# First stage with softplus spread between maxima, rows placed one batch back and TensorE's loop turned; experts on 28 pairs of tiles, then 15 single tiles

## The chip, the core and the metric

One core of a Trainium2 chip runs the whole program in one launch. The metric is the device time of that execution in microseconds. The kernel before was timed at 1516.23 us (median of three runs).

## What is computed

A block of three residual layers over 128 sequences of 32 rows of 256 numbers (4096 rows in all), in float32.

```python
x = x + cross_attention(layernorm(x), ctx)     # ctx: 128 x 257 x 256, 16 heads of 16
x = x + ssd_layer(layernorm(x))                # dt = softplus(...); cumulative sums; conv; W_out
# mixture of experts, z = layernorm(x), 8 experts, 256 -> 704 -> 256, the best 2 for each row
logits = z @ w_router.T
top_w, sel = jax.lax.top_k(logits, 2)
gates[row, sel] = softmax(top_w)
for e in range(8):
    h = silu(z @ w_gate[e]) * (z @ w_up[e])
    out = out + gates[:, e:e+1] * (h @ w_down[e])
x = x + out
```

## The kernel before

The program has two blocks, and all engines run each from lists written out by hand. Everything is ordered by semaphores: an instruction waits until a counter has reached a value. In loops the value depends on the loop's register, so a wait can cost the engine's sequencer an instruction of its own.

**First stage** (`attend`). The rows are worked in 32 tiles of 128 rows; a tile holds 4 sequences, called batches b = 0 to 3 (n = 4i + b). `steps` writes tiles 0 to 3 out, runs tiles 4 to 28 as a hardware loop of 25 turns, and writes the rest out. Several batches are in flight at once. While batch n has its values weighed (`weigh_values`, L412 with output `k`), the probabilities of n + 1 are turned (`transpose_probs`, outputs `pt` and `v_p` at L476), and keys and values of n + 2 are projected (`project_k`, `project_v`, outputs `k` and `v_p`). The scores (output `sc`) of n + 1 stand at the head of batch n's piece of the list. Between these stand small steps of the layers behind (`turn_a`, `turn_b`, `turn_c`: outputs `m`), one per gap. Each matmul of a context or expert product is done three times, high by high, high by low and low by high part (fp32r operands), so that the result is nearly float32.

VectorE takes the maximum of each group of scores (`maxima`, L884), copies the keys out of PSUM (`take_keys`, L873), takes reciprocals (L891), and does the small vector work of the other layers: softplus by a series in L977 to L1003 (its last product, L1003, gives `a_done`, which TensorE's scores of batch 1 wait for, since the series has its scratch in the second bank of scores), the placement of routed rows in L1080 to L1102 (`place`), queries in L923 and the layer norms. ScalarE does the exponentials and PSUM copies, GpSimd the low parts of the context (`ctx_lo`), the powers and the indirect DMAs; SyncE issues plain DMAs.

At the end `plan_tiles` works out on VectorE which expert each tile of 128 table rows belongs to, in a chain of 10 small operations, and writes it to `info`.

**Second stage** (`experts`). 71 tiles of up to 128 routed rows, each of one expert, run two per loop turn (`tiles`, `body`). For each tile GpSimd copies the tile's column of the table (`gi`, `oi` at L1664), gathers the rows by an indirect DMA (L1670) and later adds the result to the output by another (L1676, `scatter`, which waits until the one before has landed); TensorE turns the rows (`z_p`, L1480, 2 transposes), multiplies them by the gate and up weights (`gate_p`, `up_p`: rows stationary, weights moving, 24 matmuls of 352 columns), turns the product `h` (`ht_p`, L1513, 6 transposes), and multiplies by the down weights (`y_p`, 18 matmuls of 256 columns). ScalarE and VectorE split the weights of the tile's expert into high and low parts anew for every tile (`gw`, `uw`: L1553 on ScalarE, L1611 on VectorE, 1408 numbers a partition each). The low part of the down weights comes by DMA (768 KB a tile).

Of the kernel before, what the change touches and what calls it, by code (L numbers as in the profile page):

```python
# [4 lines left out]
F32 = mybir.dt.float32  # L5
# [7 lines left out]
P = 128  # L13
# [20 lines left out]
NSLOT = (TOK * TOPK + E * (P - 1)) // P  # L34
assert NSLOT % 2 == 1
# [42 lines left out]
def perceiver(nc, xd, ctxd, ctxl, maskd, pard, wxbcd, cond, padd, wgd, wud, wdd, outd):  # L78
# [5 lines left out]
    with keep:  # L84
# [8 lines left out]
        info = keep.enter_context(nc.sbuf_tensor("info", [P, 2, NSLOT + 1], I32))  # L93
# [21 lines left out]
def attend(nc, xd, ctxd, ctxl, maskd, pard, wxbcd, cond, padd, wgd, wud, wdd, d_high, d_low, zbuf, table, outd, con, cst, wg, wu, wd,  # L115
# [7 lines left out]
    with own:  # L123
# [11 lines left out]
        cnti = sb("cnti", [P, E], I32)  # L135
        past = sb("past", [P, 2, E])
        tl = sb("tl", [P, 5])
# [134 lines left out]
        PLAN = 10  # L272
# [137 lines left out]
        def _(pe):  # L410
# [15 lines left out]
            def project_k(i, b):  # L426
# [4 lines left out]
                at_least(pe, k_done, 2 * n)  # L431
                at_least(pe, ou_done, n - 2)
                at_least(pe, rp_done, n - 2)
# [7 lines left out]
            def project_v(i, b):  # L441
                n = 4 * i + b
                hi, lo = ctx_hi[:, b % 2], ctx_lo[:, b % 2]
                at_least(pe, v_done, n)
                at_least(pe, pt_done, 2 * n - 2)
# [7 lines left out]
            def scores(i, b):  # L453
                n = 4 * i + b
                pe.wait_ge(qbd_done, n + 1)
                pe.wait_ge(k_done, 2 * n + 2)
                pe.wait_ge(last_done, n + 1)
                at_least(pe, max_done, 4 * n)
# [8 lines left out]
            def transpose_probs(i, b, d):  # L467
                n = 4 * i + b
                pe.wait_ge(exp_done, 4 * n + 2 * d + 2)
                at_least(pe, pt_done, 2 * n)  # L470
# [8 lines left out]
            def weigh_values(i, b):  # L479
                n = 4 * i + b  # L480
                pe.wait_ge(pt_done, 2 * n + 2)
                pe.wait_ge(v_done, n + 1)
                if runs(following(i, b, 2)[0]):
                    pe.wait_ge(k_done, 2 * n + 6)
                at_least(pe, ou_done, n)
                at_least(pe, rp_done, n)
# [181 lines left out]
            def tile(i):  # L668
                for b in range(TB):
                    nxt, two = following(i, b), following(i, b, 2)  # L670
                    if runs(nxt[0]):
                        scores(*nxt)
# [10 lines left out]
                    if runs(nxt[0]):  # L683
                        transpose_probs(*nxt, 1)

# [14 lines left out]
            turn_z1(1)  # L700
            steps(pe, tile)
# [4 lines left out]
            for k in range(2):  # L706
                last = mm(M[0:1, (k + 1) * P:(k + 2) * P], tl[:, 3 + k:4 + k], ident)
# [156 lines left out]
        def _(dve):  # L864
# [104 lines left out]
            def link(ins, j, k):  # L969

                ins.then_inc(soft, 1)
                dve.wait_ge(soft, NSOFT * j + k)

            def softplus_ratio(j):
                dve.wait_ge(u_done, j + 1)
                dve.wait_ge(soft_max, j + 1)
                link(V.tensor_scalar(sr, su, 2.0, None, ALU.add), j, 1)  # L977
                link(V.reciprocal(ss, sr), j, 2)
                V.tensor_tensor(sy, su, ss, ALU.mult).then_inc(soft, 1)
                V.tensor_tensor(sp_y, su, ss, ALU.mult).then_inc(soft, 1)  # L980

            def softplus_series(j, first, last):

                if first == 0:
                    dve.wait_ge(soft, NSOFT * j + 4)
                    link(V.tensor_tensor(sw, sp_y, sy, ALU.mult), j, 5)
                    V.tensor_scalar(ss, sw, 1.0 / ATANH[0], None, ALU.mult).then_inc(soft, 1)
# [117 lines left out]
            def plan_tiles():  # L1105
# [3 lines left out]
                def link(ins):  # L1109
                    k[0] += 1  # L1110
                    ins.then_inc(plan, 1)
                    if k[0] < PLAN:
                        dve.wait_ge(plan, k[0])

                number = cst("tok")[:, 0:1]
                dve.wait_ge(cnt_ready, 1)
                link(V.tensor_scalar(cnti[:, :], M[:, 0:E], float(P - 1), None, ALU.add))
                link(V.tensor_scalar(cnti[:, :], cnti[:, :], P.bit_length() - 1, None, ALU.logical_shift_right))
                link(V.tensor_copy(cnt[:, 0, :], cnti[:, :]))
                link(V.tensor_tensor_scan(cnt[:, 1, :], ones[:, 0:E], cnt[:, 0, :], 0.0, ALU.mult, ALU.add))  # L1120

                link(V.tensor_scalar(past[:, 0, :], cnt[:, 1, :], number, None, ALU.is_le))
                link(V.tensor_tensor(past[:, 1, :], past[:, 0, :], cnt[:, 0, :], ALU.mult))
                link(V.tensor_reduce(tl[:, 0:2], past[:, :, :], AX.X, ALU.add))
                link(V.tensor_tensor(tl[:, 2:3], number, tl[:, 1:2], ALU.subtract))
# [637 lines left out]
```

## Time and profile before

| | us |
|---|---|
| median of 3 runs | 1516.23 |
| lowest, highest | 1511.95, 1516.65 |
| the profiled execution, its own time | 1514.07 |
| its span, first to last instruction | 1512.0 |
| TensorE busy | 1418.8 (94%) |
| VectorE, ScalarE, GpSimd busy | 1119.2, 1002.8, 833.8 |

The page cuts the span into 40 equal slices; the first stage reaches to about 1000 us, the experts follow. TensorE's matmuls are pipelined, so a matmul's duration is longer than its turn: starts of successive matmuls give the pace. Durations are of one execution, on one core.

### The profile page before, as it was taken

What the parts mean: (1) busy time and instruction counts of PE and PEld (TensorE: products, weight loads), DVE (VectorE), ACT (ScalarE), POOL (GpSimd) and SP (SyncE); (2) the same over time, 40 slices, a digit from 0 to 9 for tenths busy, and PEclk for the clock granted to TensorE, in tenths of its full rate; (3) what the DMA queues carried; (4) which work ended last, traced back from release to release, by engine and by line L of the source; (5) the groups of instructions that cost most, each with busy time, mean ns of one, the idle gap of its engine ahead of it and who ended that gap; (6) DMA issues with size and microseconds to landing.
All of it is one profiled execution on the core that took longest, in us unless ns stands there. A gap on an engine that the chain in (4) does not pass through costs nothing.

```text
span 1512.0 us, 54304 instructions
## 1 busy us (share of the span) xinstructions
PE 1418.8 (94%) x15668; PEld 1285.3 (85%) x15669; DVE 1119.2 (74%) x3999; ACT 1002.8 (66%) x2482; POOL 833.8 (55%) x1401
## 2 busy tenths in 40 slices
PE   6969999999999999999999999559999999999997
PEld 5858888888888888888888888459999999999997
DVE  3647877877877877877877877558777777787775
ACT  4626777677777767767767766147767677677674
POOL 3514655655655665665665654236666656566554
PEclk9969999999999999999999999569999999999999
DMA  6202454454343343343343231425555555555554
GB/s 189 71 21 72 139 180 129 145 186 129 104 112 91 100 116 91 97 119 91 92 120 95 83 83 31 183 97 145 160 145 151 155 143 159 136 144 162 143 143 111
DMA packets 102009, 183.81 MB, mean 122 GB/s; under 512 B 19392, under 2 KB 61376, under 8 KB 101792
## 3 DMA queue, kind: packets, MB, share of 16 engines
q1 hardware_dynamic: 86272, 164.35, 35.8%
q0 software_dynamic: 15680, 18.76, 7.0%
q8 instruction: 29, 0.48, 0.1%
q14 instruction: 28, 0.23, 0.0%
HBM read 152.63 MB, written 31.13 MB: 122 GB/s over the span
## 4 chain that ended last, share of the span: by engine, by line
PE 70%; DVE 10%; issue 7%; DMA 2%; POOL 2%; ACT 1%; DVEq 1%; POOLq 0%; ACTq 0%; SPq 0%
PE k L412 12%; PE m L412 10%; PE y_p L1474 9%; PE up_p L1474 9%; PE gate_p L1474 8%; PE v_p L412 6%; PE sc L412 5%; PE v_p L476 4%; PE pt L476 3%; PE ht_p L1513 3%; DVE kT L873 2%; DMA par<-zbuf,gi 2%; PE m L497 2%; DVE z L1031 1%; PE z_p L1480 1%
## 5 line engine op out<-in xcount | busy, mean ns | idle before, releaser
L738 ACT ACTIVATE wd<-wd,nmx 128x257 f32<-128x257 f32 x512 | 256.3, 504 | 35.3 <-DVE nmx L884 30.6
L714 ACT ACTIVATE wd<-v_p 128x512 f32<-128x512 f32 x256 | 152.6, 596 | 180.8 <-PE k L412 146.3
L884 DVE CUSTOM_DVE_ANT_0 wd<-sc,wd 128x257 f32<-128x257 f32 x512 | 192.2, 423 | 74.2 <-PE sc L412 69.5
L1301 POOL TENSOR_TENSOR ctx_lo<-wd,ctx_hi 128x516 fp32r<-128x516 f32 x128 | 166.9, 1304 | 138.3 <-ACT ctx_hi L714 138.3
L1676 POOL DMA_INDIRECT out<-par,oi x71 | 113.6, 1599 | 144.8 <-ACT par L1582 140.0
L412 PE MATMUL k<-ctx_hi,wkh 128*128 128x256 f32 x512 | 159.0, 311 | 1.7 <-POOL ctx_lo L1301 1.4
L1553 ACT ACTIVATE uw_hi<-wu 128x1408 fp32r x71 | 98.4, 1385 | 83.7 <-PE up_p L1474 83.4
L1664 POOL COPY oi<-par 128x4 int32 x71 | 148.1, 2086 | 0.0
L1611 DVE TENSOR_TENSOR uw_lo<-wu,uw_hi 128x1408 fp32r<-128x1408 f32 x71 | 115.5, 1626 | 41.2 <-ACT uw_hi L1553 41.2
L412 PE MATMUL k<-ctx_lo,wkh 128*128 128x256 f32 x512 | 145.4, 284 | 0.0
L412 PE MATMUL k<-ctx_hi,wkl 128*128 128x256 f32 x512 | 144.7, 283 | 0.0
L1611 DVE TENSOR_TENSOR gw_lo<-wg,gw_hi 128x1408 fp32r<-128x1408 f32 x71 | 115.4, 1625 | 39.2 <-ACT gw_hi L1553 39.2
L412 PE MATMUL v_p<-wvh,ctx_lo 128*128 128x256 f32 x512 | 143.8, 281 | 0.0
L412 PE MATMUL v_p<-wvh,ctx_hi 128*128 128x256 f32 x512 | 143.4, 280 | 0.0
L412 PE MATMUL v_p<-wvl,ctx_hi 128*128 128x256 f32 x512 | 142.8, 279 | 0.0
L873 DVE TENSOR_SCALAR kT<-k,par 128x256 f32<-128x256 f32 x256 | 114.0, 477 | 31.1 <-PE k L412 30.4
L1664 POOL COPY gi<-par 128x4 int32 x71 | 122.4, 1723 | 9.2 <-issue 5.6
L1474 PE MATMUL y_p<-wd,hT_hi 128*128 x426 | 120.8, 284 | 1.9 <-DVE hT_lo L1611 1.9
L1474 PE MATMUL y_p<-wd,hT_lo 128*128 x426 | 120.1, 282 | 0.0
L1474 PE MATMUL y_p<-dl,hT_hi 128*128 128x256 f32 x426 | 119.8, 281 | 0.0
L1319 POOL TENSOR_TENSOR rr<-wd,rr 128x4 f32<-128x4 f32 x128 | 25.7, 201 | 165.4 <-DVE rr L891 165.1
L1553 ACT ACTIVATE gw_hi<-wg 128x1408 fp32r x71 | 98.1, 1382 | 13.9 <-PEq L123 8.8
(200 smaller groups left out, 4719.2 us busy)
## 6 DMA issues: line engine op xcount, KB each, us to landing
dl<-d_low SPq DMA_DIRECT2D x71, 768.0 KB, 4.4
wd<-in_ctx SPq DMA_DIRECT2D x128, 258.0 KB, 2.8
wd<-in_mask SPq DMA_DIRECT2D x512, 32.1 KB, 1.8
wd<-in_wd SPq DMA_DIRECT2D x24, 256.0 KB, 3.0
d_high<-wd SPq DMA_DIRECT2D x24, 256.0 KB
d_low<-wd SPq DMA_DIRECT2D x24, 256.0 KB
wd<-d_high SPq DMA_DIRECT2D x8, 768.0 KB, 9.2
wg<-in_wg SPq DMA_DIRECT2D x8, 704.0 KB
```

The costliest lines, as they stand in the source:

```text
L412: return nc.tensor.matmul(out, lhsT, rhs, start=start, stop=stop)
L476: last = nc.tensor.transpose((PT, V_)[d][:, o:o + P], pr[:, g, t * P:(t + 1) * P], ident)
L714: return nc.scalar.activation(out, in_, ACT.Copy, **kw)
L738: nc.scalar.activation(pr[:, g, :], sm[:, g, :], ACT.Exp, bias=nmx[:, g:g + 1], scale=-1.0, accum_out=rsum[:, g:g + 1]).then_inc(exp_done, 1)
L873: V.tensor_scalar(kT[:, b % 2, a, 0:LAST], K2[:, a, :], prm("bk")[:, a:a + 1], None, ALU.add).then_inc(k_done, 1)
L884: V.tensor_tensor_reduce(sm[:, g, :], SC[g][:, 0:S], msk[:, b, :], -1.0, 3.0e38, ALU.add, ALU.min, nmx[:, g:g + 1]).then_inc(max_done, 1)
L1301: G.tensor_tensor(ctx_lo[:, b % 2], ctx[:, b], ctx_hi[:, b % 2].bitcast(F32), ALU.subtract).then_inc(lo_done, 1)
L1474: return nc.tensor.matmul(out, lhsT, rhs, start=start, stop=stop)
L1553: nc.scalar.activation(dst, src, ACT.Copy).then_inc(done, 1)
L1611: V.tensor_tensor(dst, src, hi.bitcast(F32), ALU.subtract).then_inc(done, 1)
L1664: G.tensor_copy(dst.unsqueeze(1), tab[:, bass.ds(col, 1), :]).then_inc(done, 1)
L1676: G.indirect_dma_start(outd[:, :], bass.IndirectOffsetOnAxis(oi[:, s, 1:2].bitcast(U32), 0), yb[:, s, :], None, compute_op=ALU.add).then_i ...
```

## The change

The change has four parts.

1. **TensorE's loop is turned.** In the first stage's list the scores of batch n + 2 now stand at the end of batch n's piece, and the scores of (0, 1) are written ahead of the tiles. The order of matmuls stays as it was; only the place in it where the loop branches back moves, from ahead of the scores to behind them. Waits that other waits imply are left out.
2. **Softplus is spread.** In batch 3 VectorE's softplus chain (`softplus_ratio`, `softplus_series`) is cut so that each of its first steps stands between two maxima or key copies, and the rest of the series stands behind the key copies.
3. **`place` goes from batch 2 to batch 1**, ahead of `normalise2`.
4. **Experts in pairs.** The first 28 steps of the second stage take two tiles of one expert (256 rows); 15 single tiles follow, by the code of before with other buffers. `plan_tiles` gives both lists in 25 operations. In a pair the weights are stationary and the 256 rows move: 5 full chunks of 128 hidden units (12 matmuls of 256 columns each) and a short one, gate and up side by side (6 matmuls). The product comes out with hidden units on partitions, so `h` is not turned. The weights are split once for a pair. The down product has 36 matmuls of 256 columns.

```diff
             def tile(i):                     # TensorE, first stage
                 for b in range(TB):
                     nxt, two = following(i, b), following(i, b, 2)
-                    if runs(nxt[0]):
-                        scores(*nxt)
                     turn_c(*((i, b - 1) if b else (i - 1, TB - 1)))
...
                     if runs(nxt[0]):
                         transpose_probs(*nxt, 1)
+                    if runs(two[0]):
+                        scores(*two)
...
                     if runs(nxt[0]):          # VectorE, first stage
                         maxima(*nxt, 0, 1)
                     if soft_now:
-                        softplus_ratio(i - 1)
+                        softplus_add(i - 1)
                     if runs(nxt[0]):
                         maxima(*nxt, 2)
                     if soft_now:
-                        softplus_series(i - 1, 0, 1)
+                        softplus_inverse(i - 1)
                     if runs(nxt[0]):
                         maxima(*nxt, 3)
+                    if soft_now:
+                        softplus_ratio(i - 1)
...
-                    if b == 2 and runs(i - 3):
-                        place(i - 3)
...
+                    if b == 1 and runs(i - 3):
+                        place(i - 3)
...
+            def chunk(p, s, k):               # TensorE, experts
+                at_least(pe, hf_done, FC * p + k - 2)
+                (zh, zl), (wh, wl) = zT2[s], w2
+                for side in range(1 if k == FULL else 2):
+                    o = 2 * k * P + side * P
+                    for c in range(NH):
+                        for j, (w, z) in enumerate(((wh, zh), (wh, zl), (wl, zh))):
+                            last = mm(G2[k % 3][:, side * F2:(side + 1) * F2], w[:, c, o:o + P], z[:, c, :],
+                                      c == 0 and j == 0, c == NH - 1 and j == 2)
+                last.then_inc(gu_ready, 1)
...
+            def body2(p, s):
+                chunk(p, s, 0)
+                chunk(p, s, 1)
+                if not (isinstance(p, int) and p == 0):
+                    down_pair(p - 1, 1 - s)
+                if final(p):
+                    turn_z(0, 0)
+                else:
+                    turn_pair(p + 1, 1 - s)
+                for k in range(2, FC):
+                    chunk(p, s, k)
...
+            def take_y2(p, s, h):             # ScalarE
+                act.wait_ge(yp_ready, 2 * p + h + 1)
+                act.wait_ge(oi_done, p + 1)
...
+            def scatter_pair(p, s):           # GpSimd
+                for h in range(2):
+                    held(pool, (tab_in, 16), (oi_done, p + 1), (yp_done, 2 * p + h + 1), (y_out, 16 * (2 * p + h)))
+                    G.indirect_dma_start(outd[:, :], bass.IndirectOffsetOnAxis(oi[:, s, h, 1:2].bitcast(U32), 0),
+                                         yb2[:, h, :], None, compute_op=ALU.add).then_inc(y_out, 16)
```

For each chunk of a pair ScalarE takes silu of the gate half from PSUM (`silu2`), VectorE multiplies by the up half (`gate_up2`), ScalarE rounds the product to its high part (`high_h`) and VectorE takes the low part (`low_h`); each step waits for the one before.

TensorE's list at the head of the loop of the first stage, before the change (`v_p` at L476 is the last transpose of batch 3, the branch is L282, `sc` the scores of the next tile's batch 1):

```order
L476 MATMUL v_p<-con,wd 128x128 [waits v_done,pt_done,exp_done]
L476 MATMUL v_p<-con,wd 128x128 x3
L282 REGISTER_ALU
L282 COMPARE_AND_BRANCH
L412 MATMUL sc<-kT,qbd 64x257 [waits max_done,last_done,a_done,k_done,qbd_done]
L412 MATMUL sc<-kT,qbd 64x257 x7
L412 MATMUL m<-dtv,con 128x16 [waits a_done,z1T_done]
```

The same place in the changed kernel, whose lines are numbered anew:

```order
L484 MATMUL v_p<-con,wd 128x128 [waits v_done,exp_done]
L484 MATMUL v_p<-con,wd 128x128 x3
L466 REGISTER_ALU
L420 MATMUL sc<-kT,qbd 64x257 [waits a_done,last_done,k_done]
L420 MATMUL sc<-kT,qbd 64x257 x7
L290 REGISTER_ALU
L290 COMPARE_AND_BRANCH
L420 MATMUL m<-dtv,con 128x16 [waits a_done,z1T_done]
```

The branch has moved behind the scores, and the scores have two waits fewer.

VectorE's list in batch 3, around the key copies, before (L884 maxima, L979 to L990 softplus, L873 the two key copies):

```order
L979 TENSOR_TENSOR dtv<-dtv,sc 128x16 [waits soft]
L980 TENSOR_TENSOR sc<-dtv,sc 128x16
L884 ISA wd,nmx<-sc,wd 128x257 [waits s_ready,init]
L884 ISA nmx 128x1
L986 TENSOR_TENSOR dtv<-sc,dtv 128x16 [waits soft]
L987 TENSOR_SCALAR sc<-dtv 128x16 [waits soft]
L884 ISA wd,nmx<-sc,wd 128x257 [waits s_ready,init]
L884 ISA nmx 128x1
L990 SCALAR_TENSOR_TENSOR sc<-sc,dtv 128x16 [waits soft]
L873 TENSOR_SCALAR kT<-k,par 128x256 [waits k_ready,s_ready]
L990 SCALAR_TENSOR_TENSOR sc<-sc,dtv 128x16 [waits soft]
L873 TENSOR_SCALAR kT<-k,par 128x256 [waits k_ready,s_ready]
```

And after (L892 maxima, L988 to L1002 softplus, L881 key copies, L899 the reciprocals):

```order
L892 ISA wd,nmx<-sc,wd 128x257 [waits s_ready,init]
L892 ISA nmx 128x1
L988 TENSOR_TENSOR dtv<-dtv,sc 128x16 [waits soft]
L989 TENSOR_TENSOR sc<-dtv,sc 128x16
L881 TENSOR_SCALAR kT<-k,par 128x256 [waits k_ready,s_ready]
L993 TENSOR_TENSOR dtv<-sc,dtv 128x16 [waits soft]
L881 TENSOR_SCALAR kT<-k,par 128x256 [waits k_ready,s_ready]
L999 TENSOR_SCALAR sc<-dtv 128x16 [waits soft]
L1002 SCALAR_TENSOR_TENSOR sc<-sc,dtv 128x16 [waits soft] x2
L899 RECIPROCAL rr<-rsum 128x4 [waits px_done,exp_done]
L1002 SCALAR_TENSOR_TENSOR sc<-sc,dtv 128x16 [waits soft] x4
```

Of the chain from the ratio (L979, now L988) on, six operations stood ahead of the second key copy; now three do, and seven follow it.

GpSimd's list of one single-tile step in the loop of the experts, before (L1664 the copies of the table's columns into `gi` and `oi`, L1670 the gather, L1676 the scatter):

```order
L1664 COPY oi<-par 128x4
L75 REGISTER_ALU
L1663 ISA [waits zT_ready]
L1663 TENSOR_LOAD info
L1663 ISA x2
L1664 ISA
L1664 COPY gi<-par 128x4
L66 REGISTER_ALU
L1670 DMA par<-zbuf,gi 128x256 [waits gi_done,tab_in]
L66 REGISTER_ALU
L1676 DMA out<-par,oi 4224x256 [waits y_done,y_out,oi_done,tab_in]
```

And of one pair step, after (L2007 the gathers, L1999 the copy into `oi`, L2014 the scatters):

```order
L68 REGISTER_ALU
L2007 DMA par<-zbuf,gi 128x256 [waits gi_done,tab_in]
L2007 DMA par<-zbuf,gi 128x256
L1998 ISA
L1998 TENSOR_LOAD info
L1998 ISA x2
L1999 ISA
L1999 COPY oi<-par 128x8
L68 ISA
L2014 DMA out<-par,oi 4224x256 [waits yp_done,y_out,oi_done,tab_in]
L68 ISA
L2014 DMA out<-par,oi 4224x256 [waits yp_done,y_out,oi_done,tab_in]
```

Before, a step had a copy of each kind, one gather and one scatter; now it has the same two copies, twice as wide, two gathers and two scatters, and the second scatter waits until the first has landed (`y_out`).

## Rows read from the trace of the kernel before

**Rows 1.** Two windows, one in each stage: span, then busy us per engine, clock, DMA.

```profile
500.00:900.00 400.00, 390.52 (x5308) 339.12 (x5307) 314.42 (x1554) 282.04 (x869) 233.93 (x492) 1.00 0.35 99
...
1000.00:1500.00 500.00, 489.92 (x3524) 485.94 (x3525) 387.75 (x423) 353.49 (x493) 299.02 (x278) 0.99 0.55 145
```

**Rows 2.** Timeline of TensorE in a looped tile: start, us, instructions, idle before.

```profile
608.13 0.66 PE L476 MATMUL pt<-con,wd 128*128 128x128 f32 x4
...
608.98 0.62 PE L412 MATMUL m<-par,z2T 128*128 128x16 f32 x4 [0.19 <-DVE wd L923]
...
614.46 0.65 PE L412 MATMUL k<-wd 128*32 128x64 f32 x32 [0.20 <-DVE kT L873]
...
616.00 0.63 PE L476 MATMUL v_p<-con,wd 128*128 128x128 f32 x4
...
616.88 0.69 PE L412 MATMUL sc<-kT,qbd 32*64 32x257 f32 x16 [0.26 <-issue]
...
622.29 0.66 PE L476 MATMUL pt<-con,wd 128*128 128x128 f32 x4
...
622.78 0.29 PE L412 MATMUL m<-dtv,con 128*128 128x16 f32 x2
```

**Rows 3.** The same view in a tile written out after the loop.

```profile
872.12 0.63 PE L476 MATMUL v_p<-con,wd 128*128 128x128 f32 x4
...
872.68 0.69 PE L412 MATMUL sc<-kT,qbd 32*64 32x257 f32 x16
```

**Rows 4.** Timeline of VectorE over the tile of rows 3.

```profile
858.09 0.41 DVE L1037 TENSOR_SCALAR z<-x,mv,rs 128x256 f32<-128x256 f32 x1 [1.58 <-POOL rs L1285]
...
863.19 0.16 DVE L1080 TENSOR_REDUCE sv<-ohr 128x2 f32<-128x16 f32 x1
...
864.26 0.15 DVE L1102 SCALAR_TENSOR_TENSOR ri<-ri,sv 128x2 int32<-128x2 int32 x1
...
870.05 0.48 DVE L873 TENSOR_SCALAR kT<-k,par 128x256 f32<-128x256 f32 x1
...
872.25 0.16 DVE L1003 TENSOR_TENSOR dtv<-sc,par 128x16 f32<-128x16 f32 x1
```

**Rows 5.** Timeline of TensorE over one expert tile.

```profile
1202.22 0.28 PE L1474 MATMUL y_p<-wd,hT_hi 128*128 x1
...
1204.36 0.82 PE L1513 MATMUL ht_p<-con 128*128 128x128 f32 x6
...
1205.18 0.32 PE L1474 MATMUL gate_p<-gw_lo,zT_hi 128*128 128x352 f32 x1
...
1206.79 0.32 PE L1474 MATMUL gate_p<-gw_hi,zT_lo 128*128 128x352 f32 x1
...
1207.33 0.32 PE L1474 MATMUL up_p<-uw_lo,zT_hi 128*128 128x352 f32 x1
...
1211.24 0.82 PE L1513 MATMUL ht_p<-con 128*128 128x128 f32 x6
```

**Rows 6.** Waits of TensorE in the expert stage: us in total, times, longest.

```profile
PE z_p L1480 <- DMA par<-zbuf,gi: 6.6, 4, 2.9
```

**Rows 7.** Groups of the expert stage: busy us, mean ns, idle before.

```profile
L1611 DVE TENSOR_TENSOR hT_lo<-ht_p,hT_hi 128x256 fp32r<-128x256 f32 x71 | 29.4, 415 | 0.0
...
L1553 ACT ACTIVATE hT_hi<-ht_p 128x256 fp32r<-128x256 f32 x71 | 26.9, 379 | 0.0
```

**Rows 8.** Timeline of GpSimd over the tile of rows 5.

```profile
1203.18 1.00 POOL L1670 DMA_INDIRECT par<-zbuf,gi  x1 [0.80 <-POOL gi L1664]
...
1205.94 1.60 POOL L1676 DMA_INDIRECT out<-par,oi  x1 [1.76 <-ACT par L1582]
...
1207.57 1.67 POOL L1664 COPY gi<-par 128x4 int32 x1
```

**Rows 9.** DMA issues by line: KB each where known, median us to landing.

```profile
out<-par,oi POOLq DMA_INDIRECT x71, 3.9
```

More of the change, by code:

```diff
@@ L1405, in experts @@
[L1405 to L1411 removed]
+        F2 = 2 * P
@@ new lines, in experts, with part, cut @@
+        FULL = FC - 1
+        GU = 2 * FULL * P + 2 * FL
+        SPLIT_A, SPLIT_B = 2, 4
+        ZW, HK, WW = 2 * NH * F2, 2 * (FC + 2) * F2, 2 * NH * GU
+        places = dict(w=WW, z0=ZW, z1=ZW, x=768, ht=HK, dl=FC * D)
+        begin, at = {}, 0
+        for name, n in places.items():
+            begin[name] = at
+            at += n
+        room = sb("room", [P, at], F32R)
+        def part(name, skip, n):
+            return room[:, begin[name] + skip:begin[name] + skip + n]
+        def cut(name, skip, *shapes):
+            out = []
+            for shape in shapes:
+                n = 1
+                for k in shape:
+                    n *= k
+                names = " ".join("abcd"[:len(shape)])
+                sizes = {"abcd"[k]: shape[k] for k in range(len(shape))}
+                out.append(part(name, skip, n).rearrange(f"p ({names}) -> p {names}", **sizes))
+                skip += n
+            return out
@@ L1437, in flat, with pairs @@
             return part.rearrange("p c n -> p (c n)")
+        def pairs(eng, body):
+            body(0, 0)
+            body(1, 1)
+            with eng.Fori(2, NPAIR - 2, 2) as p:
+                body(p, 0)
+                body(p + 1, 1)
+            body(NPAIR - 2, 0)
+            body(NPAIR - 1, 1)
         def tiles(eng, body):
@@ L1659, in _, with pair_owners, gather_pair @@
             G = nc.gpsimd
+            def pair_owners(dst, p, done):
+                col = G.value_load(info[0:1, 0, bass.ds(p, 1)], min_val=0, max_val=TCOL - 2)
+                G.tensor_copy(dst, tab[:, bass.ds(col, 2), :]).then_inc(done, 1)
+            def gather_pair(p, s):
+                if not (isinstance(p, int) and p < 2):
+                    pool.wait_ge(z_ready, p - 1)
+                pair_owners(gi[:, s], p, gi_done)
+                held(pool, (tab_in, 16), (gi_done, p + 1))
+                for h in range(2):
+                    G.indirect_dma_start(zg2[:, s, h, :], None, zbuf[:, :],
+                                         bass.IndirectOffsetOnAxis(gi[:, s, h, 0:1].bitcast(U32), 0)).then_inc(zg_in[s], 16)
```

518 lines of the change are left out of this document (382 added, 136 removed).

## The prediction

> **What bounds the kernel now.** I read the table of windows first, to see whether each stage has one limit. It has: TensorE is busy 390.5 of 400 us in a stretch of the first stage and 489.9 of 500 in one of the experts, at full clock, while VectorE has 314 and 388, ScalarE 282 and 353, GpSimd 234 and 299 [rows 1]. So an edit pays by matmul time that it takes out, or by the small holes between matmuls. I looked for those in TensorE's timeline, taking starts of successive groups, because matmuls overlap. Then VectorE's timeline, for what is late ahead of each hole; then the experts' timeline of TensorE and of GpSimd, whose serial loop is the nearest other limit of a pair.
>
> **Turned loop.** Where the loop branches, the scores start 0.88 us after the last value transposes (616.00 to 616.88) [rows 2]; in a tile written out, with the same matmuls and no branch, 0.56 [rows 3]. The branch costs 0.32. Behind the scores it has their 0.69 us of matmuls to hide under; I leave 0.1 exposed, since it still has to be fetched and the next instruction waits on counters. The Trainium skill ("Advanced Engine Details and Errata", "Control Flow Timing") puts a compare-and-branch at about 108 ns; by that the part would give some 3 us over 25 turns, not 8. The rows show three times that, and they decide, since the branch brings register work with it. The dropped waits I cost at nothing: with or without a branch, the 0.56 holds them.
>
> **Softplus spread.** TensorE waits 0.20 for the keys at 614.46 [rows 2], because six softplus operations stand ahead of VectorE's second key copy. With three there, that is gone. What is late next is the end of the series: the product at L1003 ended at 872.41, and the scores of batch 1 wait for it, which started 872.68 (872.25 + 0.16) [rows 3, 4]. The slack is 0.27 there, and about 0.59 in the loop, where the branch held the scores back. VectorE's work ahead of that product is the same, so it ends when it did, and with 0.32 and 0.20 taken from TensorE's way only 0.07 of slack is left. I give 0.05 back for it. Boundary: 0.32 + 0.20 - 0.1 - 0.05 = 0.37; 25 turns make 9.3 us. In the written-out tiles only the key wait goes, some 0.1 each, 0.7 in all.
>
> **Place moved.** In batch 2 the queries of L923 are late, because `place` (863.19 to 864.41, 1.2 us [rows 4]) stands ahead: from `pt` to the next group 0.85 us instead of the usual 0.49 (608.13 to 608.98, against 622.29 to 622.78) [rows 2], so 0.36 are lost a tile. In batch 1 it goes ahead of the normalise, before which VectorE stands idle for 1.58 us waiting for GpSimd's powers [rows 4]: 1.2 fits, if its own inputs are there. That idle is the cover; without it the 1.2 would delay L1037 and, two groups on, TensorE. Of the 0.36 I take 0.24, since the value transposes wait for ScalarE's copy anyway: 28 tiles, 6.7 us. In the last tiles, where the pipeline is thin, `place` also leaves the chain: 1 to 2 us. **First stage: 9.3 + 0.7 + 6.7 + 1.3 = 18.** Bounds: 5 (only half of each hole comes free) and 25 (all of 0.52 and 0.36, 13 + 10, and the tail).
>
> **Pairs.** One tile takes 6.88 us of TensorE (`ht_p` to `ht_p`, 1204.36 to 1211.24), two 13.76. From the rows: 18 down matmuls of 256 columns start over 2.14 us (1202.22 to 1204.36), 0.119 each. Gate matmuls of 352 columns take 0.161 (ten from 1205.18 to 1206.79). The 0.54 to the first up matmul hold two of these and two transposes: 0.22 for the transposes. The six transposes of `h` take 0.82 - 0.16 = 0.66 [rows 5].
> A pair has 5 x 12 + 6 = 66 matmuls of 256 columns for gate and up, and 36 for down: 102 x 0.119 = 12.14. Four transposes of rows: 0.44. Sum 12.6; the saving is 1.16 a pair, of which 2 x 0.66 is turned `h` that no longer exists; the columns that stream are as many as before (102 x 256 = 26,112 = 2 x (24 x 352 + 18 x 256)). Times 28: -32.5 us. That is the ceiling.
> What eats of it: each chunk of 1.43 us (12 x 0.119) has a chain behind it of silu, product, high part, low part, four steps that I price by the 256-wide 379 ns of ScalarE and 415 ns of VectorE [rows 7]: about 1.6 us plus hand-offs. Three buffers of PSUM let it lag two chunks, 2.86 us, and the last chunk's chain must be over within chunks 0 and 1 of the next pair. It fits, by about a microsecond at each chunk and by some 0.3 at the end if VectorE and ScalarE have weight splits queued. Neither engine gets fuller: VectorE was busy 78% of the stretch, 10.7 us for two tiles, ScalarE 71%, 9.7 [rows 1], and the split of the weights is now done once instead of twice.
> GpSimd is closer. Its cycle for a pair is serial: first scatter issued, landed, second scatter issued, then a copy of `gi`, two gathers, a copy of `oi`. With 1.6 a scatter, 1.0 a gather [rows 8], 3.9 from issue to landing [rows 9], 0.8 idle ahead of a gather [rows 8], about 0.5 for ScalarE's last evacuation and 0.9 of waiting and issue at each scatter (half of the 1.76 there [rows 8], the rest being ScalarE's lateness), and 2.35 for the two gathers: 0.5 + 0.9 + 3.9 + 0.9 + 1.6 + 0.8 + 2.35 = 10.95, and two copies. A copy can last 0.2 or 1.67 [rows 8]: 11.3 to 14.4. TensorE gives it 12.6. I take a pace of 12.8: (13.76 - 12.8) x 28 = **-27**.
> Why a copy of 4 numbers takes 1.67 us only sometimes, the profile doesn't say. The Trainium skill ("SBUF — State Buffer", "SBUF: two separate sides") has the port that VectorE and GpSimd share as an exclusive lock, held for the whole of a VectorE operation with two SBUF inputs while GpSimd reads SBUF. By that rule more of them in a pair speak against this change. The long copy fits it, the trace doesn't prove it; with both copies long the cycle is 14.4 and the pairs lose half a microsecond each.
>
> **Gathers, start, transition.** TensorE waited 6.6 us for gathers in four places [rows 6]; 43 steps with the gather a longer step ahead keep perhaps 1.5: -5. Against that the start of the experts is later by about 2 (a second gather of 1.0 ahead of the first matmul, wider splits of weights, four transposes for two). From the last pair to the first single tile its last chain (about 1.6 plus hand-offs) has no chunks to hide under, then the single tile starts cold: +3.5. Fifteen single tiles run as before. `plan_tiles` has 15 operations more of about 0.15 us (the small ones of [rows 4]), covered by the table's way to memory and back; uncovered they are +2.
>
> **Sum.** -18 - 27 - 5 + 2 + 3.5 = -44.5. The profiled execution took 1514.07 us: 1469.6. The median lies 2.2 above it, so I say 1472.
>
> **Rivals.**
> A, the forecast: TensorE sets the pace of pairs at 12.6 to 12.9, first stage -10 to -25: 1460 to 1480 (at best, all bounds together and start and transition at 3: 1516 - 25 - 32.5 - 6.6 + 3 = 1455). Chance 0.55.
> B, pairs paced by GpSimd's serial cycle at 13.0 to 13.7. For: two scatters that wait for one another, one of two copies long. Against: TensorE's 12.6 lies above the low half of the cycle's range, and an expert's gather runs a pair ahead. 28 x 0.5 = 14 less saved: 1475 to 1495. 0.25.
> C, the first stage gives nothing: the end of softplus (L1003) takes the place of the branch and the keys. For: it ended 0.27 ahead of the scores [rows 3, 4], and nothing moves it forward. Against: the 0.36 of `place` is another batch. With pairs dense: 1516.2 - 27 - 5 + 5.5 = 1490. 0.10.
> D, slower: the cycle of B passes 13.76, the time of two single tiles. It needs both copies long and the scatter's landing above 3.9 on wide pairs. The first stage and the gathers bring 23, less 2 + 3.5 is 17.5, so the sign turns at a cycle of 13.76 + 17.5 / 28 = 14.4; at 15.5 the pairs lose 28 x 1.74 = 49, less 17.5: about 1547. 0.06. Between 14.2 and 14.55 it is no change that can be told: 0.04.
>
> **Numbers.** Likeliest: 1472. A measurement of this kernel tells about 0.3% from no change, 4.5 us. Faster 0.90 (A, B, C), same 0.04, slower 0.06. For 8 in 10 the range takes A, most of B and C: 1453 to 1500.
>
> **What would show it.** After: `sc` at the head of batch 1 about 0.56 behind the last `v_p` and the branch's hole under 0.15 behind it; `k<-wd` without a wait for `kT`; L923's wait gone, and L1037 no later than before. In the experts 28 pairs 12.6 to 12.9 apart with TensorE's waits on silu and low parts under 0.2 each; if they are further apart, the chain of waits goes through `yb2`, the scatters and the `oi` copy (B, D), or through `hf_done` (the chunks' chain). Wrong would be: 12.6 missed with GpSimd idle, which would mean that the hand-offs of chunks are dearer than 0.3; or a first stage that didn't move.

## The result: 1.3% faster, less than half of what was forecast

The changed kernel took 1496.84 us (median of 4), the kernel before 1516.44: a ratio of 0.9873 with a 95% interval of 0.9855 to 0.9891, 19.6 us less. The forecast was 1472, 44 us less. The profiled execution has a span of 1494.8 us.

The windows of the changed kernel, in the columns of [rows 1]: one in the first stage, one in the pairs.

```profile
500.00:900.00 400.00, 399.44 (x5480) 351.91 (x5478) 328.01 (x1604) 290.32 (x906) 240.62 (x505) 1.00 0.36 99
1000.00:1340.00 340.00, 329.17 (x2571) 311.56 (x2570) 220.46 (x460) 215.19 (x509) 142.65 (x145) 1.00 0.40 94
```

The first stage is denser than before (399.4 of 400 us against 390.5), the pairs are not (329.2 of 340 is 96.8%, against 98.0% of before). So the change gained in one stage and lost in the other. Laid on a clock (the profiled execution of each kernel): TensorE's first gate matmul of the experts came at 1003.0 us before and at 976.6 now, 26.4 earlier. The experts then took, from there to the start of the last matmul, 502.2 us before and 512.5 now, 10.3 more. That makes 16.1; the end behind the last matmul is 1.1 shorter, which gives the 17.2 between the two spans, and the rest to 19.6 is the difference between single executions and medians.

**First stage.** TensorE's timeline in a looped tile, the places of [rows 2]:

```profile
593.47 0.66 PE L484 MATMUL pt<-con,wd 128*128 128x128 f32 x4
593.96 0.52 PE L420 MATMUL m<-par,z2T 128*128 128x16 f32 x4
594.33 0.64 PE L484 MATMUL v_p<-con,wd 128*128 128x128 f32 x4
...
599.07 0.65 PE L420 MATMUL k<-wd 128*32 128x64 f32 x32
...
599.70 0.65 PE L484 MATMUL pt<-con,wd 128*128 128x128 f32 x4
...
600.61 0.63 PE L484 MATMUL v_p<-con,wd 128*128 128x128 f32 x4
601.17 0.69 PE L420 MATMUL sc<-kT,qbd 32*64 32x257 f32 x16
601.79 0.40 PE L420 MATMUL m<-dtv,con 128*128 128x16 f32 x2
```

No wait is left in it. The queries' group follows `pt` after 0.49 us (0.85 before), the keys' group has no wait for `kT`, and the scores follow the value transposes after 0.56 (0.88 before). The first matmul behind the branch follows the scores after 0.62, which is the scores' own length: the branch has gone out of sight wholly. Matmul by matmul, a turn is shorter by 0.33 us at the branch, 0.27 at the keys and 0.46 at the queries, and lasts 27.37 instead of 28.47.

VectorE's timeline around the moved `place` (L1092 to L1114) and the normalise behind it:

```profile
612.96 0.14 DVE L1092 TENSOR_REDUCE sv<-ohr 128x2 f32<-128x16 f32 x1
...
614.16 0.15 DVE L1114 SCALAR_TENSOR_TENSOR ri<-ri,sv 128x2 int32<-128x2 int32 x1
614.64 0.41 DVE L1049 TENSOR_SCALAR z<-x,mv,rs 128x256 f32<-128x256 f32 x1 [0.33 <-POOL rs L1314]
```

Its 1.35 us fill the idle time that stood ahead of the normalise: 1.58 in [rows 4], 0.33 here.

**Pairs.** TensorE's timeline over one pair, from the transposes of the next pair's rows to those of the one after:

```profile
1109.08 0.66 PE L1605 MATMUL all_p<-con,par 128*128 128x128 f32 x4
1109.49 8.15 PE L1596 MATMUL all_p<-room 128*128 128x256 f32 x66
1118.38 0.38 PE L1596 MATMUL all_p<-wd,room 128*128 x1 [0.74 <-DVE room L1884]
...
1120.12 0.59 PE L1596 MATMUL all_p<-wd,room 128*128 x2
1120.55 0.28 PE L1596 MATMUL all_p<-room 64*128 64x256 f32 x1
1120.67 0.59 PE L1596 MATMUL all_p<-wd,room 64*128 x2
1121.10 0.28 PE L1596 MATMUL all_p<-room 128*128 128x256 f32 x1
...
1122.63 0.59 PE L1596 MATMUL all_p<-wd,room 128*128 x2
...
1123.39 0.66 PE L1605 MATMUL all_p<-con,par 128*128 128x128 f32 x4
```

A pair lasts 14.31 us here and 13.8 in the next one; the two lengths alternate, with a mean of 14.05 over twenty pairs. Before, two single tiles took 13.76 [rows 5]. Two things were not in the forecast's sum. First, ahead of the down product TensorE waits 0.74 us for VectorE's low part of `h` (L1884). Second, matmuls of 64 rows stand in the down product. Where the count of active rows changes, the start lies 0.21 us behind the one before, and the one after that again 0.22, instead of 0.12 (1120.12, a group of two of which the second is the first of 64 rows, then 1120.55, in the rows "64*128"). Added up from start to start over 17 pairs, a pair has 12.6 us of matmuls and transposes as forecast, 0.74 for four changes of rows, 0.58 of waits, and 0.1 of rest.

**Ends of the pairs.** TensorE's timeline from the last pair to the single tiles:

```profile
1369.10 0.38 PE L1596 MATMUL all_p<-wd,room 128*128 x1 [2.57 <-DVE room L1884]
...
1379.58 0.85 PE L1694 MATMUL all_p<-con 128*128 128x128 f32 x6 [1.10 <-issue]
...
1388.00 0.69 PE L1612 MATMUL all_p<-con,par 128*128 128x128 f32 x2 [5.66 <-DMA par<-zbuf,gi]
```

There are three waits of 2.57, 1.10 and 5.66 us, 9.3 together, where 3.5 were allowed for. The chain of work that ended last names the third:

```profile
1373.07 6.47 DMA out<-par,oi
...
1382.62 1.70 POOL gi L2032
...
1385.14 2.81 DMA par<-zbuf,gi
...
1388.00 0.69 PE all_p L1612 x2
```

In GpSimd's list the gather for single tile 2 stands behind the last pair's two scatters, and the second of these waits for the first to land (6.47 us, where [rows 9] have a median of 3.9).

**GpSimd in the pairs**, its timeline over the same pair:

```profile
1110.31 1.63 POOL L2014 DMA_INDIRECT out<-par,oi  x1 [2.80 <-ACT par L1781]
1114.96 1.58 POOL L2014 DMA_INDIRECT out<-par,oi  x1 [3.02 <-DMA out<-par,oi]
1115.98 0.77 POOL L1999 COPY gi<-par 128x8 int32 x1
1117.58 1.02 POOL L2007 DMA_INDIRECT par<-zbuf,gi  x1 [0.83 <-POOL gi L1999]
1118.90 1.36 POOL L2007 DMA_INDIRECT par<-zbuf,gi  x1 [0.30 <-issue]
1120.27 0.51 POOL L1999 COPY oi<-par 128x8 int32 x1
1124.66 1.63 POOL L2014 DMA_INDIRECT out<-par,oi  x1 [3.88 <-ACT par L1781]
```

From the first scatter to the end of the `oi` copy are 10.5 us, and then it is idle for 3.88, waiting for ScalarE's scaled rows. Its serial cycle does not set the pace, and the copies are short (0.77 and 0.51; 1.67 in [rows 8]).

### The profile page after: what moved, and what is told of

It reads as the page before. It is cut to its first block, busy times and chain, and to the rows that moved or that the text cites. A ratio compares the mean times of both kernels' runs of the same rounds, so it can differ in the third digit from the quotient of the medians.

```text
span 1494.8 us, 53378 instructions
## 1 busy us (share of the span) xinstructions
PE 1404.7 (94%) x15840; PEld 1263.0 (84%) x15841; DVE 1071.7 (72%) x4211; ACT 964.0 (64%) x2678; POOL 756.3 (51%) x1345
## 4 chain that ended last, share of the span: by engine, by line
PE 81%; issue 3%; DVE 3%; ACT 2%; DMA 2%; POOL 1%; DVEq 1%; POOLq 0%; ACTq 0%; SPq 0%
PE all_p L1596 26%; PE k L420 16%; PE m L420 12%; PE v_p L420 11%; PE sc L420 5%; PE pt L484 4%; PE v_p L484 4%; PE m L504 2%; PE all_p L1605 1%; DMA par<-zbuf,gi 1%; ACT room L1731 1%; DVE con L1913 1%; DVE room L1884 1%; DMA out<-par,oi 0%; DVEq L1922 0%
## 5 line engine op out<-in xcount | busy, mean ns | idle before, releaser
L1596 PE MATMUL all_p<-room 128*128 128x256 f32 (+1 forms) x2634 | 415.8, 292 | 1.8 <-issue 1.5
L1596 PEld LDWEIGHTS all_p<-room 128*128 128x128 f32 x2634 | 364.2, 193 | 2.6 <-issue 2.3
L892 DVE CUSTOM_DVE_ANT_0 wd<-sc,wd 128x257 f32<-128x257 f32 x512 | 191.4, 421 | 63.6 <-PE sc L420 57.4
L2014 POOL DMA_INDIRECT out<-par,oi x56 | 89.7, 1602 | 208.2 <-ACT par L1781 106.1
L1596 PE MATMUL all_p<-wd,room 128*128 (+1 forms) x852 | 177.2, 294 | 16.2 <-DVE room L1884 13.9
L1596 PEld LDWEIGHTS all_p<-wd,room 128*128 128x128 f32 (+1 forms) x852 | 138.9, 188 | 33.2 <-issue 21.8
L881 DVE TENSOR_SCALAR kT<-k,par 128x256 f32<-128x256 f32 x256 | 114.1, 477 | 24.6 <-PE k L420 23.9
L1731 ACT ACTIVATE room<-con 128x256 fp32r<-128x256 f32 x168 | 70.1, 418 | 88.1 <-DVE con L1913 88.0
L1884 DVE TENSOR_TENSOR room<-con,room 128x256 fp32r<-128x256 f32 x168 | 71.1, 423 | 57.3 <-ACT room L1731 55.1
L1884 DVE TENSOR_TENSOR room<-wg,room 128x512 fp32r<-128x512 f32 (+3 forms) x99 | 78.6, 794 | 43.5 <-ACT room L1731 43.5
L420 PEld LDWEIGHTS k<-ctx_hi,wkh 128*128 128x128 f32 x512 | 97.6, 191 | 5.3 <-issue 2.9
L420 PEld LDWEIGHTS k<-ctx_lo,wkh 128*128 128x128 f32 x512 | 97.9, 191 | 0.9
L420 PEld LDWEIGHTS k<-ctx_hi,wkl 128*128 128x128 f32 x512 | 97.8, 191 | 0.0
```

What stands on the lines that cost most here:

```text
L420: return nc.tensor.matmul(out, lhsT, rhs, start=start, stop=stop)
L881: V.tensor_scalar(kT[:, b % 2, a, 0:LAST], K2[:, a, :], prm("bk")[:, a:a + 1], None, ALU.add).then_inc(k_done, 1)
L892: V.tensor_tensor_reduce(sm[:, g, :], SC[g][:, 0:S], msk[:, b, :], -1.0, 3.0e38, ALU.add, ALU.min, nmx[:, g:g + 1]).then_inc(max_done, 1)
L1596: return nc.tensor.matmul(out, lhsT, rhs, start=start, stop=stop)
L1731: nc.scalar.activation(dst, src, ACT.Copy).then_inc(done, 1)
L1884: V.tensor_tensor(dst, src, hi.bitcast(F32), ALU.subtract).then_inc(done, 1)
```

## The experiments

Times are medians, and "before beside it" is the kernel before, timed with the run on the same chip. "turn" is the period of TensorE's list in a looped tile, "pair" is the mean period of a pair, and "experts" the time from the first gate matmul to the last matmul's start, all from the trace. The kernel before has 28.47 and 502.2, the changed one 27.38 and 512.5.

| run | us | before beside it | turn | pair | experts |
|---|---|---|---|---|---|
| e_rows, e_rows2 | 1493.9, 1498.1 | 1516.5, 1517.2 | 28.13, 28.20 | 13.33 | 494.3, 493.5 |
| e_vload | 1500.0 | 1516.5 | 28.13 | 13.56 | 502.0 |
| e_turn, e_turn2 | 1499.5, 1482.2 | 1516.5, 1516.0 | 28.13, 27.39 | 13.51 | 500.9, 500.3 |
| e_both, e_both2 | 1487.8, 1487.1 | 1516.5, 1517.2 | 28.14, 28.19 | 13.08 | 485.3, 487.5 |
| e_best | 1482.4 | 1517.2 | 28.16 | 13.08 | 481.5 |
| e_swap | 1478.2 | 1517.2 | 28.20 | 12.91 | 476.6 |
| again, again2, again3 | 1496.7, 1495.9, 1495.9 | 1516.0, 1516.9, 1515.5 | 27.37 to 27.38 | 14.06 | 514.7, 514.0, 514.7 |
| s_all, s_all2 | 1489.3, 1489.5 | 1516.0, 1516.9 | 27.54 | - | 501.6, 504.8 |
| p_only | 1524.5 | 1516.0 | 28.48 | 14.06 | 508.8 |
| x_piece | 1494.3 | 1516.9 | 27.38 | - | 513.9 |
| x_best, x_best2 | 1460.1, 1458.0 | 1516.9, 1515.5 | 27.39, 27.38 | 12.91 | 476.0, 476.4 |

### The two stages apart

`s_all` is the kernel before with the three edits of the first stage; its waits and its experts stay.

```diff
 s_all: before, and
+ scores of (n + 2) at the end of a batch's piece of TensorE's list, scores(0, 1) ahead
+ softplus cut up between maxima and key copies (b == 3)
+ place(i - 3) in b == 1
```

> The kernel before with the three edits of the first stage (turned loop, softplus spread, place moved) and its own experts. By the changed kernel's trace a loop turn loses 0.33 (branch), 0.27 (keys) and 0.46 us (place): 28.47 to 27.37, 25 turns and the rest 28 us, so about 1488. By the prediction's terms 18 us: 1498. If the shift of 0.75 us a turn shows here too: about 1507.

> The kernel before with the three edits of the first stage, once more. Theory X: turns of 28.3 and 1506 on a chip with the delay, 27.54 and 1489 on one without.

1489.3 against 1516.0: 0.9827 (0.9807 to 0.9847), and 0.9824 (0.9807 to 0.9840) the second time (`s_all2`). The three edits bring 27 us, not 18. A turn is 27.54. The 0.16 to the changed kernel's 27.38 are mostly gaps ahead of two `k<-ctx_hi` groups (0.19 and 0.10 instead of 0.11 and 0.03), where waits stand that the change leaves out: about 4 us over 25 turns, which the prediction had put at nothing.

`p_only` is the changed kernel with the first stage's lists and waits as before.

```diff
 p_only: changed kernel, and
- scores(*two) at the end, softplus spread, place in b == 1, fewer waits
+ the lists and waits of before
```

> The changed kernel with the first stage's lists as before (branch ahead of the scores, softplus and place as before), so the pairs alone. Theory: the experts cost 10 us more than before (pairs 14.06 us against 13.74, and their transition), 1526. The prediction had them 26 us cheaper: 1490.

1524.5 against 1516.0: 1.0066 (1.0042 to 1.0091). Alone, the pairs make the kernel slower. The parts make -27 - 4 + 8.5 = -22.5 together, the whole -19.6.

The experts of this trace were 4 to 6 us shorter than those of the changed kernel, and TensorE's waits for single tiles' gathers say where (us in total, times, longest; both in the stretch 1340:1512). First `p_only`, then the changed kernel:

```profile
PE all_p L1608 <- DMA par<-zbuf,gi: 0.9, 1, 0.9
```

```profile
PE all_p L1612 <- DMA par<-zbuf,gi: 6.9, 2, 5.7
```

The long wait behind the last scatters is missing in `p_only`, though the order of GpSimd's list is the same. Its four executions took 1521.4, 1521.8, 1527.2 and 1527.6 us, and the profiled one is the first. By the two longer ones the pairs cost 11.4, and the parts make -27 - 4 + 11.4 = -19.6, the whole. That the longer ones had the long wait is likely, but not shown, since they have no trace.

### What holds the pairs

```diff
 e_rows: changed kernel, and
-                        r, at = rows_of(c), slot(s, c)
+                        r, at = slice(0, P), slot(s, c)
+            V.memset(hf[1][FL:P, :], 0.0)      # once, and copied into rows 64 to 127 of the slot
```

> The changed kernel, but the last piece of the down product runs on all 128 rows (rows 64 to 127 of h are set to zero once), so TensorE never goes from 128 to 64 active rows and back inside a pair. Theory R (each change between 128 and 64 rows costs about 0.19 us, four a pair): a pair gets 0.74 us shorter, 14.06 to 13.3, the experts 21 us, the time about 1476. Rival W (the matmuls are slow there because their weights have only just been written, or because the wait ahead of them is what counts): starts stay 0.21 apart and the time stays within 3 us of 1497.

> The run with all 128 rows in the down product once more, on another chip if it comes so. If a loop turn of the first stage takes 27.4 us here, theory R gives 1476; with turns of 28.1 as in its first run, 1494 again. Rival W (the gaps at the row changes belong to something else) gives 1494 to 1497 with turns of 27.4.

The pairs got 0.72 us shorter (14.05 to 13.33), the experts 18 to 19 us, as theory R said; the starts of 0.21 are gone from the down product, so rival W is out. TensorE's timeline of `e_rows` over one down product and the transposes behind it:

```profile
1128.59 0.38 PE L1597 MATMUL all_p<-wd,room 128*128 x1 [0.96 <-DVE room L1885]
...
1131.76 0.40 PE L1597 MATMUL all_p<-wd,room 128*128 x2
...
1132.82 0.28 PE L1597 MATMUL all_p<-wd,room 128*128 x1
1132.94 0.60 PE L1606 MATMUL all_p<-con,par 128*128 128x128 f32 x4
```

36 matmuls take 4.35 us from 1128.59 to 1132.94, against 5.01 in the changed kernel (1118.38 to 1123.39), though they stream zeros on more rows. The time as a whole hardly moved, for another reason: the turn of the first stage went from 27.4 to 28.1 (below).

```diff
 e_vload: changed kernel, and on ScalarE (VectorE alike)
-                e = nc.scalar.value_load(pair_expert(p), ...)
                 if begun:
                     silu2(p - 1, FULL)
                     high_h(p - 1, 1 - s, FULL)
+                e = nc.scalar.value_load(pair_expert(p), ...)
```

> The changed kernel, but ScalarE and VectorE read the number of the next pair's expert after the last chunk's silu, product, high and low part, not ahead of them. Theory C (TensorE's wait ahead of the down product, 0.58 us a pair, is the last chunk's chain, begun late because of what stands ahead of silu): silu starts 0.26 earlier in every pair, so 28 x 0.26 = 7 us less, about 1490; the two kinds of pair (13.8 and 14.3) stay apart. Rival D (the chain is paced by the data of the DMA or by the weights' split): no change, 1497.

ScalarE's timeline of the changed kernel, at the last chunks of two pairs (L1764 silu, L1731 high part):

```profile
1114.95 0.42 ACT L1731 ACTIVATE room<-con 128x256 fp32r<-128x256 f32 x1 [0.49 <-DVE con L1913]
1116.04 0.38 ACT L1764 ACTIVATE con<-all_p 64x256 f32<-64x256 f32 x1 [0.67 <-issue]
1117.15 0.42 ACT L1731 ACTIVATE room<-con 64x256 fp32r<-64x256 f32 x1 [0.74 <-DVE con L1913]
```

```profile
1129.27 0.42 ACT L1731 ACTIVATE room<-con 128x256 fp32r<-128x256 f32 x1 [0.49 <-DVE con L1913]
1129.95 0.38 ACT L1764 ACTIVATE con<-all_p 64x256 f32<-64x256 f32 x1 [0.26 <-issue]
1130.89 0.42 ACT L1731 ACTIVATE room<-con 64x256 fp32r<-64x256 f32 x1 [0.57 <-DVE con L1913]
```

The silu of the short chunk stands 0.67 and 0.26 us behind the work ahead of it, with "issue" as the cause: its input had long been there. With the number read later, pairs are 13.62 and 13.49 us, the experts 10.5 to 12.7 shorter. Theory C holds, but it had the size wrong: it expected 7 us less and the two kinds of pair still apart. They come to within 0.13, with the loop's branch where it was, so it was the register load, not the branch, that made most of the difference.

```diff
 e_turn: changed kernel, and on ScalarE (VectorE alike)
-                if begun:
-                    silu2(p - 1, FULL)
-                    high_h(p - 1, 1 - s, FULL)
...
-                for k in range(2, FULL):
+                for k in range(2, FC):
```

> The changed kernel, but the last chunk's steps stand at the end of a pair's list on ScalarE and VectorE, so neither the expert's number nor the loop's branch comes ahead of them; the order of the work is the same. Theory C: the chain begins 0.67 earlier behind a branch and 0.26 in the other pairs, TensorE's wait of 0.58 on average is gone, pairs are all about 13.5 us: 16 us less, about 1481. Rival D: no change.

> The run with the last chunk at the end of the lists once more, beside the control on one chip. Theory Y: 1499 again, first-stage turns of 28.1. Theory X: it goes with the control, 16 us below it whatever that is.

Pairs of 13.5, both kinds, and 1482.2 against 1496.7 beside it on one chip. That is the 14.5 us of theory C (16 expected). Only 0.05 us a pair came on top of the later reading, so moving the steps ahead of the branch brought next to nothing more.

`e_both` has both edits, that of `e_rows` and that of `e_turn`.

> Both edits: all 128 rows and the last chunk at the end of the lists. Theories R and C together: a pair is 102 matmuls and four transposes back to back, 12.7 us, the time 1497 - 37 = 1460, which is what the prediction gave the pairs. Rival G (GpSimd's serial cycle of two gathers and two scatters is the next limit at 13.0 to 13.7): pairs stop at 13.0 or more and TensorE waits for rows or for the buffer of results, 1468 or more.

> Both edits of the pairs once more. With turns of 27.4 us in the first stage: 1470 (its first run's 1487.8 less 25 turns of 0.7). The pairs 12.98 us on average, as in its first run, since that does not hang on the chip.

Pairs took 13.08 us: mostly 12.75 and 13.24 in turn. So R and C add up but for 0.3 us. By the number alone rival G would fit (13.0 or more), but all that TensorE waits for in this stretch (1109:1340 of `e_both`) is the low part of `h`:

```profile
PE all_p L1597 <- DVE room L1880: 4.5, 10, 0.7
```

It has no wait for rows or for the buffer of results, so G is out.

```diff
 e_best: e_both, and on GpSimd
+            body(0, 0, first=True)             # gathers the rows of single tile 2
             pair_owners(oi[:, 1], NPAIR - 1, oi_done)
             scatter_pair(NPAIR - 1, 1)
-            body(0, 0, first=True)
```

> Both edits, and at the end of the pairs GpSimd gathers the rows of single tile 2 ahead of the last pair's two scatters, not behind them. Theory T (TensorE's wait of 5.7 us for that gather is only its place in GpSimd's list behind scatters that wait for one another): the wait goes, 3 us (the wait was 3.0 with both edits) to 5.7 less than the run with both edits, about 1466. Rival: the wait moves to the next gather or to the scatter's buffer, less than 1 us gained.

1482.4 against 1487.1, 4.7 us less. TensorE's waits for single tiles' gathers fell from 7.3 us in three places (longest 5.7) in `e_both2` to 3.2 in four (longest 1.5). Theory T holds.

```diff
 e_swap: e_best, and on ScalarE (VectorE alike)
+                silu2(p, FULL)
                 high_h(p, s, FULL - 1)
-                silu2(p, FULL)
                 high_h(p, s, FULL)
+  VectorE, first product of a pair: dve.wait_ge(h_low, FC * p - 1)
```

> As the one before, and in each pair silu and product of the short last chunk go ahead of high and low part of the chunk before it (the same work in another order; one more wait on VectorE at a pair's first product). Theory C: what is left of TensorE's wait ahead of the down product, 0.3 to 0.5 us in every second pair, is the chain still running behind; it starts 0.4 earlier: pairs of 12.75 all, 28 x 0.23 = 6 us less, about 1460. Rival: the wait is of the chunk before and moves there, or the order costs a hand-off: no gain or a loss of 3 us.

Pairs took 12.91 us, and the time is 4.2 less. The wait of 4.5 us that `e_both` had for the low part of `h` in the stretch 1109:1340 is gone, so the last chunk's chain was what was left; some 0.2 us a pair still stand above 12.7.

### A first stage that is 0.7 to 0.8 us a turn longer on some chips

In eight runs, with edits in the experts alone, a turn of the first stage took 28.1 to 28.2 us. Four of them shared one chip, four another. `e_turn` was among them with 1499.5 and took 1482.2 on a third chip. VectorE's timeline at the head of a turn, `e_turn` and then `e_turn2`, the same kernel:

```profile
609.96 0.17 DVE L1078 TENSOR_TENSOR lg<-oh 128x8 f32<-128x8 f32 x1
611.58 0.43 DVE L892 CUSTOM_DVE_ANT_0 wd<-sc,wd 128x257 f32<-128x257 f32 x1 [1.45 <-PE sc L420]
```

```profile
599.74 0.17 DVE L1078 TENSOR_TENSOR lg<-oh 128x8 f32<-128x8 f32 x1
600.55 0.43 DVE L892 CUSTOM_DVE_ANT_0 wd<-sc,wd 128x257 f32<-128x257 f32 x1 [0.65 <-PE sc L420]
```

The wait for the scores lasts 1.45 us instead of 0.65, though TensorE had them going at 609.60, 0.56 behind `v_p` as always. The lateness goes on to TensorE:

```profile
615.00 0.66 PE L484 MATMUL pt<-con,wd 128*128 128x128 f32 x4
616.16 0.40 PE L420 MATMUL m<-dtv,con 128*128 128x16 f32 x2 [0.50 <-DVE t L940]
```

It waits 0.50 there. Only the turns that load and store a piece of the down weights have it: in `e_turn` tiles 3 and 4 took 27.43 and 27.37, tiles 5 to 27 28.1, tile 28 27.45. In that stretch the trace of `e_turn` has no counter moving from 610.68 to 611.38, and SyncE's next transfer late as well.

> The changed kernel itself, as a control. In the four runs with an edit in the experts alone, the loop turns of the first stage took 28.1 us where the changed kernel took 27.37, all of it on VectorE's first maximum behind its loop branch, which got its scores' signal 0.8 us later; the pairs got shorter as expected. Theory X (it is the chip on which a run is made, not the kernel): here it takes 28.1 too and the time is about 1514. Theory Y (something in the edited kernels shifts the first stage, such as where its code or its counters lie): here it is 27.4 again and 1497.

> The changed kernel as a control. Theory X (the delay of 0.8 us a turn goes with the chip, for every kernel with the edits of the first stage): if the other three show turns of 28.1 here, this one does too and takes 1513; if they show 27.4, it shows 27.4 and 1497. Theory Y (it goes with the kernels edited in the experts): 27.4 here whatever the others show.

> The changed kernel as a control. On a chip with the delay theory X says turns of 28.1 us and a time of 1514; theory Y says 27.4 and 1497 on every chip. On a chip without the delay both say 27.4, 1497, and the question stays open.

The changed kernel had turns of 27.38 on three chips, and so had `e_turn2`, `x_piece` and `x_best` beside it. So theories X and Y were not told apart for it. `x_piece` loads the piece 8 us later in a turn:

```diff
 x_piece: changed kernel, SyncE
-                if k is not None:
-                    load_piece(k)
                 for b in range(TB):
...
+                    if b == 1 and k is not None:
+                        load_piece(k)
```

> The changed kernel, but SyncE loads the piece of the down weights 8 us later in a turn, behind the transfers of batch 1, not at the head, where two stores, a load of x, the context and four masks are under way. Theory K (the crowd at the head of the turn holds the counters up): with the delay in the control, turns fall from 28.1 towards 27.4 and the time by up to 17 us; without it in the control, no change. Rival: the delay is of GpSimd's two scatters or the context's load, and it stays.

There was no delay in the changed kernel beside it, and 1494.3 against 1495.9 is no change that can be told, so theory K was not put to the test. `x_best` joins all edits of the experts and that one.

> All the edits together: 128 rows, the last chunk at the end, its silu and product first, the gather ahead of the scatters, and the piece's load 8 us later. Turns of 27.4 and experts of 476.6 us as in the run before: 1461. If the delay stays: 1478.

> All edits with the piece's load moved, once more. On a chip with the delay theory K says turns near 27.4 and 1460, its rival 28.2 and 1478. On a chip without it 1460 again.

1460.1 and 1458.0: ratios 0.9635 (0.9619 to 0.9651) and 0.9629 (0.9613 to 0.9645). This is the fastest kernel of the study, 38 us below the changed one, but on two chips without the delay. The same `e_turn` had the delay on one chip and not on another; each was one run, so it may be the chip or something else that differed between them. Whether it hits the changed kernel, and what it is, stays open. For that reason the comparisons above are of experts' times or of runs beside one another.

## Why the prediction was wrong

**The step that failed is "Pairs"**, in two of its terms. "Sum 12.6; the saving is 1.16 a pair" took 102 matmuls at 0.119 us each, whatever their rows. That price was right for the 128-row ones, but the changed kernel's down product takes `rows_of(c)`, 64 rows in the last piece, where the kernel before had every down matmul on 128 rows (the shape 128*128 of `y_p` in [rows 5]). The four changes cost 0.74 us a pair by the starts, 0.72 by `e_rows`. The Trainium skill ("TensorEngine Tiling (Array Packing)", "Key Properties") says that a change of tiling mode drains TensorE. The traces fit that if going from 128 to 64 rows is such a change, with 0.1 us more on each of two starts; that a drain is the mechanism, they do not show. The prediction did not weigh that rule.

The other term is the chain of the last chunk: "It fits ... by some 0.3 at the end". It missed: TensorE waited 0.58 us a pair on average. Durations were priced rightly (silu 0.38, product 0.42, high 0.42, low 0.43), but the prediction left out that ScalarE reads the next pair's expert number ahead of the last silu: a register load that the profile counts as "issue", 0.26 to 0.67 us. The two make 1.32 us on top of 12.6; the 0.2 that was allowed for GpSimd was not needed. So the term of -27 measured 28 x (14.05 - 13.76) = +8. The prediction's own sign of being wrong, "12.6 missed with GpSimd idle", came true, but the reading it gave, dearer hand-offs of chunks, covers neither the rows nor the register load.

**Gathers, start, transition.** The start cost 1.3 us (2 expected): from the last small matmul that counts the routed rows to the first gate matmul 17.4 us (959.16 to 976.60) against 16.1 (986.88 to 1002.99). TensorE's waits for gathers fell from 6.6 us [rows 6] to 1.2 outside the transition, as said. But the transition took 9.3 us, not 3.5: the first wait of 2.57 was the last chain without cover, which was forecast (about 1.6 plus hand-offs), the 5.66 were the gather of tile 2 behind the scatters, a place in GpSimd's list that the prediction did not look at. `e_best` took 4.7 back. Pairs, gathers and transition make 8 - 5.4 + 9.3 = 11.9, and 10.3 were measured.

**First stage.** The mechanisms were right, each at its place, and the size too small: 18 forecast, and 27 by `s_all`, without the dropped waits, which bring about 4 more. In the profiled execution the first gate matmul came 26.4 earlier, although the experts' start had grown by 1.3. Each is above the upper bound of 25. None of the three deductions came true. The branch has no 0.1 left over behind the scores, the end of softplus gives nothing back, and `place` brings 0.46 where 0.24 was taken, since the transposes behind the queries start earlier with them. Rival C is refuted.

**Rivals.** B and D were about GpSimd's cycle: it is 10.5 us of 14, idle 3.9 in the pair shown. (The cycle's upper end is 10.95 + 2 x 1.67 = 14.3, not the 14.4 of the prediction; nothing hangs on it.) A copy of 1.67 us did not come again in the pairs. The rule of the Trainium skill on the shared port ("SBUF — State Buffer", "SBUF: two separate sides") is neither shown nor refuted by that: copies of `gi` lasted 0.75 to 0.95 in the pairs from 1109 to 1340 us. D's outcome, pairs dearer than two single tiles, came by another way: `p_only` is slower than the kernel before.

The time landed inside 1453 to 1500 by luck, through two errors of opposite sign. To the first gate matmul 16 us less were forecast (18, less 2 for the start) and 26.4 measured; from there to the last matmul 28.5 less were forecast (27 + 5 - 3.5) and 10.3 more measured.

## What to carry to other kernels

When a product is cut into pieces, count in the diff which of its matmuls change their number of rows, and price each change on both sides, or fill the short piece with zero rows: that took 18 to 19 us off the experts here. Where an engine has to finish a chain for another, look at what its sequencer does ahead of the chain's first instruction, register loads above all. And three holes between matmuls, each with one cause in the trace, came back whole when the cause went: deduct only what a row shows.

## What the runs showed of the hardware

A matmul of 64 rows behind one of 128, or the other way round, starts 0.21 us after it, and the next one 0.22 after that, where 0.12 is usual (matmuls of 256 columns, weights of 128 columns, full clock). Down products with the short piece took 5.01 us, with zero rows 4.35.

A register load from SBUF ahead of an activation stood as 0.26 us of "issue" idle, 0.67 behind a loop's branch. Reading the number later, on ScalarE and VectorE, took 10.5 to 12.7 us off the experts of 28 pairs.

A loop's branch, with its register work, cost TensorE 0.33 us a turn where it stood between two matmuls, and nothing with 0.62 us of matmuls queued ahead of it.

One and the same kernel (`e_turn`) took 1499.5 us on one chip and 1482.2 on another, with turns of 28.13 and 27.39 us, while the kernel before took 1516.5 and 1516.0 beside it. That its waits hide the delay would fit, but no trace of it with the delay was taken.
